# Attention scores of two batches on 32x64 TensorE tiles, probabilities turned in the score banks, row sum divided at the output's eviction

## The chip, the cores and the metric

The kernel runs on one core of a Trainium2 chip. The metric is the device time of one execution in microseconds. Five engines take part: TensorE (PE; its weight loads are PEld), VectorE (DVE), ScalarE (ACT), GpSimd (POOL) and SyncE (SP), each with its own queue of instructions, tied together by semaphores.

## The reference

Four residual steps on x of 128 batches x 32 tokens x 256 channels:

```python
x = x + einsum('bct,bcd->bdt', x, w0[cond])          # a 32x32 matrix for each batch
x = x + attention(x)                                 # paged keys and values, window of 128
x = x + einsum('bct,bcd->bdt', x, w2[subj])
x = x + x @ W.T + s[a] * (x @ A[a].T) @ B[a].T        # a = adapter of the batch
```

The attention has 8 query heads in 4 groups (G = 4, two heads a group), a head dimension of 32, and blocks of 16 keys:

```python
q, k, v = x @ Wq.T, x @ Wk.T, x @ Wv.T; q, k = rope(rms(q)), rope(rms(k))
k_blocks[blk, :, off] = k; v_blocks[blk, :, off] = v  # the new tokens are written first
scores = einsum('bghtd,bgsd->bghts', q, k_all[table]) * SCALE
allowed = (kpos <= pos) & (kpos > pos - WINDOW)
p = softmax(where(allowed, scores, -inf))
out = einsum('bghts,bgsd->bghtd', p, v_all) @ Wo.T
```

All of it is fp32. Only the 11 blocks that the window can touch are read, KEYS = 176 keys a batch.

## The kernel before

A first part (to about 118 us) works out indices on VectorE and GpSimd, applies w0, projects queries, keys and values of all 32 tiles (a tile is 4 batches x 32 tokens = 128 rows), spills x and q to memory, and scatters new keys and values into a buffer of written blocks. Then it gathers, in groups of 8 batches, old and newly written blocks (`gather_old`, `gather_new`, indirect DMAs of GpSimd).

The second part is a software pipeline written by hand. `run_slots` calls, on each engine, `slot(it, k)`: k runs from -8 to 138, with k = 8 to 23 as the body of a loop of six turns (16 slots each, a "pass" below), and the rest unrolled. Slot k works on batch k's scores, batch k-1's transposed probabilities, batch k-2's product with the values, and, by tables, on end steps of earlier tiles and preparation of the next group. On TensorE slot k is, in order:

- `s_exp` of batch k-2 awaited, then the scores of batch k: for each of two heads h of a group, one fp32 matmul of all 128 rows (4 groups x 32 dimensions) with a block-diagonal query `qbd` as weights (128 columns, 4 groups x 32 tokens), and one bf16 matmul of `mask_sel` with the penalty tile `pen` that adds the mask (L1328, L1329)
- one end step (`FIN`): x2 (output projection, slots 3 mod 4), x3 (w2, 0 mod 4), xa (adapter's A, 1 mod 4), x4 (W and B, 2 mod 4)
- four transposes of batch k-1's normalised probabilities into another bank (L1339)
- preparation (`PREP`): four transposes of keys (L1287, four times a group) or two of queries (L1279, twice a group)
- eight matmuls with the values for batch k-2, each 88 keys by a group's 32 columns, over 64 columns of probabilities (L1354); the four groups g write at four column tiles

An fp32 matmul is two records in the trace (L1328 has four of them a slot for two matmuls); a transpose is one.

VectorE in slot k takes the maximum of batch k (L704), copies keys, rotates queries, makes the penalty of the next tile (`make_pen`, in slots 3 mod 4, used from the next slot on), reorders gathered blocks, adds x2 (L735) or masks xa (L738, which x4 then waits for), and only then waits for the slot's exponentials, takes the reciprocal (L744) and scales the probabilities (L749, two instructions). ScalarE evicts the output (L1113) and the end steps, computes the two exponentials with their row sums (L1130), and copies the transposed probabilities out (L1143) and the turned queries into the block diagonal (L1153, four copies).

```python
PREP = {0: [("k0", None)], 1: [("k1", None)], 2: [("k2", None)], 3: [("qT", 0)], 4: [("k3", None)], 7: [("qT", 1)]}
FIN = {3: ("x2", 7), 0: ("x3", 8), 1: ("xa", 9), 2: ("x4", 10)}
```

`k0` waits for the gather of the newly written blocks (L871); SyncE's store of the values (L991) waits for the same gather. GpSimd starts the gather of a group in slot 1 of the group before, after the instruction `rstd` (L828), which VectorE's rotation of queries releases in slot 0 (L576).

## Time and profile before

| what | us |
|---|---|
| median of 3 runs | 558.14 |
| the three runs | 554.74, 558.14, 560.75 |
| span of the profiled execution | 556.0 |
| TensorE busy in it | 466.1 |
| VectorE busy | 413.0 |
| ScalarE busy | 341.7 |
| slot 0 starts on TensorE | 167.9 |
| last instruction of slot 127's scores | about 540 |

The profiled execution's own time is known by its span alone; the median of the runs lies 2.1 us over it. Busy time is a sum over all stages. The 128 slots between 168 and 540 us are two thirds of the span, so what a change of the slot is worth is read there.

### The profile page before, as it was taken

To read this page: it belongs to the slowest core of one execution; us is meant where nothing else is said; L and a number is where in the kernel's file an instruction comes from. 1 tells how busy PE (TensorE), PEld (TensorE's weight loads), DVE (VectorE), ACT (ScalarE), POOL (GpSimd) and SP (SyncE) were. 2 spreads that over 40 slices of the span, in tenths; PEclk is the share of its full clock that TensorE was granted. 3 is DMA by queue.
4 is the path that set the end of the run, shared out by engine and by line. 5 is a ranking of instruction groups with operands and counts; after the bars stand their busy time and mean duration, and the time that the engine had idled before them with its cause. 6 is when DMAs were issued, how large, how long until landed. Compare 5 with 4: busy or idle time off the path is not lost.

```text
span 556.0 us, 15369 instructions
## 1 busy us (share of the span) xinstructions
PE 466.1 (84%) x4726; PEld 386.1 (69%) x4726; DVE 413.0 (74%) x1357; ACT 341.7 (61%) x1075; POOL 205.6 (37%) x236
## 2 busy tenths in 40 slices
PE   0648899980015999999999999999999999999996
PEld 0537799970014688778778877877887887888884
DVE  7965577954116888888888878888888888788651
ACT  6238454455004677677777777768677775877662
POOL 7422588979603132332314324152331423211000
PEclk9999999995557899999999999999999999999999
DMA  7977776658266575757667596875858769645000
GB/s 231 293 271 306 242 219 203 201 176 199 67 155 144 146 179 150 171 142 182 155 132 179 129 174 159 151 175 124 181 139 134 182 144 182 153 127 128 13 21 19
DMA packets 97784, 90.09 MB, mean 162 GB/s; under 512 B 22967, under 2 KB 93655, under 8 KB 94972
## 3 DMA queue, kind: packets, MB, share of 16 engines
q1 hardware_dynamic: 82384, 52.58, 38.6%
q0 software_dynamic: 9312, 31.58, 22.1%
q10 hardware_dynamic: 6056, 5.54, 3.0%
q8 instruction: 16, 0.26, 0.2%
q14 instruction: 16, 0.13, 0.1%
HBM read 78.02 MB, written 35.65 MB: 204 GB/s over the span
## 4 chain that ended last, share of the span: by engine, by line
issue 47%; PE 12%; POOL 10%; DMA 3%; POOLq 1%; ACT 1%; DVE 0%; ACTq 0%; DVEq 0%
POOL old L862 4%; PE bank L1328 3%; DMA new<-written_blocks,g_idx 3%; POOL new L871 3%; POOL rms L828 3%; PE bank L1339 2%; PE bank L1354 2%; PE bank L1311 1%; POOL g_idx L855 1%; PE bank L1292 1%; PE bank L1306 1%; PE bank L1312 1%; PE bank L1329 1%; PE bank L1300 1%; PE bank L1287 0%
## 5 line engine op out<-in xcount | busy, mean ns | idle before, releaser
L828 POOL TENSOR_TENSOR rms<-rms,halfpow 128x8 f32<-128x8 f32 x48 | 86.1, 1793 | 247.4 <-DVE rms L576 247.4
L1130 ACT ACTIVATE p_room<-bank,nmax 128x176 f32<-128x176 f32 x256 | 101.4, 403 | 79.0 <-DVE nmax L704 74.9
L1328 PE MATMUL bank<-blocks_room,qbd 128*128 128x176 f32 x512 | 127.1, 352 | 6.6 <-issue 5.5
L1328 PEld LDWEIGHTS bank<-blocks_room,qbd 128*128 128x128 f32 x512 | 78.5, 193 | 26.6 <-issue 7.8
L1339 PE MATMUL bank<-ident,p_room 128*88 128x128 f32 x512 | 77.9, 275 | 4.8 <-DVE p_room L749 4.2
L704 DVE TENSOR_REDUCE nmax<-bank 128x2 f32<-128x352 f32 x128 | 66.6, 521 | 20.4 <-PE bank L1329 17.6
L1143 ACT ACTIVATE pT_room<-bank 88x512 f32<-88x512 f32 x128 | 75.1, 587 | 0.4 <-PE bank L1339 0.4
L749 DVE TENSOR_SCALAR p_room<-p_room,rrec 128x176 f32<-128x176 f32 x256 | 70.1, 316 | 5.6
L1339 PEld LDWEIGHTS bank<-ident,p_room 128*88 128x88 f32 x512 | 57.5, 123 | 15.9 <-DVE p_room L749 8.7
L712 DVE COPY blocks_room<-bank 128x352 f32<-128x352 f32 x64 | 47.5, 747 | 22.2 <-PE bank L1287 22.2
L1329 PE MATMUL bank<-pen,mask_sel 128*128 128x176 bf16 x256 | 61.9, 242 | 0.0
L1287 PE MATMUL bank<-ident,new 88*128 88x88 f32 x256 | 31.4, 249 | 34.3 <-DMA new<-written_blocks,g_idx 34.0
L1130 ACT ACTIVATION_READ_ACCUMULATOR p_room<-bank,nmax 128x1 f32 x256 | 51.5, 201 | 0.0
L1287 PEld LDWEIGHTS bank<-ident,new 88*128 88x128 f32 x256 | 26.7, 147 | 35.7 <-DMA new<-written_blocks,g_idx 35.0
L1153 ACT ACTIVATE qbd<-bank 32x256 f32<-32x256 f32 x128 | 47.4, 371 | 1.1
L1124 ACT ACTIVATE end_room<-bank 128x256 f32<-128x256 f32 x32 | 12.3, 383 | 57.8 <-PE bank L1312 57.8
L744 DVE RECIPROCAL rrec<-rsum 128x2 f32<-128x2 f32 x128 | 20.3, 159 | 34.1 <-ACT p_room L1130 33.7
L847 POOL DMA_INDIRECT written_blocks<-blocks_room,kv_idx x32 | 34.9, 1090 | 13.5 <-issue 13.5
L1311 PE MATMUL bank<-w3T,end_room 128*128 128x256 f32 x128 | 35.1, 397 | 1.8 <-DVE end_room L738 0.5
L1292 PE MATMUL bank<-woT,end_room 128*128 128x256 f32 x128 | 34.0, 388 | 0.6 <-ACT end_room L1124 0.6
L1231 PE MATMUL bank<-wkvT,pT_room 128*128 128x256 f32 x128 | 33.8, 388 | 0.0
L1077 ACT ACTIVATE blocks_room<-bank 128x256 f32<-128x256 f32 x32 | 12.3, 384 | 34.9 <-PE bank L1233 30.1
(199 smaller groups left out, 938.4 us busy)
## 6 DMA issues: line engine op xcount, KB each, us to landing
values_by_group<-new SPq DMA_DIRECT2D x16, 704.0 KB
blocks_room<-values_by_group SPq DMA_DIRECT2D x8, 704.0 KB
v_room<-values_by_group SPq DMA_DIRECT2D x8, 704.0 KB
xin<-in_x_dram SPq DMA_DIRECT2D x32, 128.0 KB
x_spill<-v_room SPq DMA_DIRECT2D x32, 128.0 KB
q_spill<-v_room SPq DMA_DIRECT2D x32, 128.0 KB
written_blocks<-new ACTq DMA_DIRECT2D x2, 2048.0 KB, 8.7
blocks_room<-q_spill SPq DMA_DIRECT2D x32, 128.0 KB
```

The source lines that it names most:

```text
L704: v.tensor_reduce(nmax[:, k % 4, :], ps_s[k % 2][:, 0:HPG * KEYS].rearrange("p (h k) -> p h k", h=HPG), AX.X, ALU.max, negate=True).then_i ...
L712: v.tensor_copy(kT[n % 2][:, :, :, o:o + 4].rearrange("p f w o -> p o f w"), ps_m[bank][:, 0:4 * ROWS].rearrange("p (o f w) -> p o f w", o ...
L749: last = v.tensor_scalar(pn[k % 2][:, h, :], pex[k % 2][:, h, :], rrec[:, k % 4, h:h + 1], None, ALU.mult)
L828: pool.tensor_tensor(out=rms[:, i, 2, :], in0=rms[:, i, 1, :], in1=halfpow[:, :], op=ALU.pow).then_inc(s_rstd, 1)
L1130: last = a.activation(pex[k % 2][:, h, :], ps_s[k % 2][:, h * KEYS:(h + 1) * KEYS], ACT.Exp, bias=nmax[:, k % 4, h:h + 1], accum_out=rsum[ ...
L1143: a.activation(pT[(k - 1) % 2][:, :, :, :].rearrange("p c h t -> p (c h t)"), ps_p[(k - 1) % 2][0:HK, :], ACT.Copy).then_inc(s_ptc, 1)
L1153: last = a.activation(qbd[n // 2 % 2][rows, TB * (n % 2):TB * (n % 2) + TB, :, C * g:C * g + C], m[rows, 0:HPG * 128].rearrange("p (h f t) ...
L1287: last = turn_over(m[:, ROWS * o:ROWS * o + ROWS], new[i][0:ROWS, o0 + o, 0, :], ident[0:ROWS, 0:ROWS])
L1311: mm(m[:, 0:T], x3T[n % 2][:, c, :], w3T[:, c, :], start=(c == 0), stop=False)
L1328: mm(dst, qbd[grp % 2][:, f, h, :], kT[grp % 2][:, f, :, :].rearrange("p w o -> p (w o)"), start=True, stop=False)
L1329: last = mm(dst, mask_sel[:, k % 4, :], pen[n % 2][:, :], start=False, stop=True)
L1339: last = turn_over(ps_p[(k - 1) % 2][0:HK, (HPG * c + h) * 128:(HPG * c + h + 1) * 128], pn[(k - 1) % 2][:, h, HK * c:HK * c + HK], ident[ ...
```

## The change

A slot no longer handles one batch with all four groups, but a *unit*: two batches (f2 = 0, 1) with two of the four groups (i = 0, 1; g = 2 (k mod 2) + i). Two slots still make two batches. Its parts:

- The query is kept compact (`qT`, 128 rows x 64 columns a batch) in place of the block diagonal. For each i and f2 one fp32 matmul works on a tile of 32 rows (the group's dimensions) and 64 columns (heads x tokens) at partitions 64 f2, in bank i of a pair of banks. The mask is added first, by two bf16 matmuls over the whole array.
- The four transposes of the unnormalised probabilities go back into the same pair of banks, which the scores no longer need. The scores of slot k+2 so wait for the copy out of these banks (`s_ptc`), where they waited for the exponentials.
- The scaling on VectorE is gone. Once in two slots it takes a reciprocal of four row sums and spreads it to 128 columns (`rrep`), TensorE turns that into half a bank (`s_nt`), ScalarE copies it (`norm`) once in four slots, and VectorE multiplies the output by it while evicting to `oT`.
- The matmuls with the values cycle over two column tiles a slot.
- The order in a slot: on TensorE the transposes now stand ahead of the end step, and on ScalarE copy and exponentials stand ahead of the end step's copies and the reordering. The memsets of `qbd` and the copies into the diagonal are gone (one copy of 128x256 in place of four of 32x256).

```diff
-        mask_sel = sb("mask_sel", [128, TB, 128], bf16)
+        mask_sel = sb("mask_sel", [128, 2, 128], bf16)
...
-        qbd = [sb(f"qbd{i}", [128, GB, HPG, 128]) for i in range(2)]
+        qT = [sb(f"qT{i}", [128, GB, HPG, C]) for i in range(2)]
...
-        rsum = sb("rsum", [128, 4, HPG])
-        rrec = sb("rrec", [128, 4, HPG])
-        ps = [ctx.enter_context(nc.psum_tensor(f"bank{i}", [128, 512], f32)) for i in range(8)]
-        ps_s, ps_p, ps_o, ps_m = ps[0:2], [ps[2], ps[4]], ps[5], [ps[6], ps[7], ps[3]]
+        rsum = sb("rsum", [128, 2, G])
+        rrec = sb("rrec", [128, 2, G])
+        rrep = sb("rrep", [128, 2, G * HD])
+        norm = [sb(f"norm{i}", [128, TB * HPG * C]) for i in range(2)]
+
+        ps_u = [ctx.enter_context(nc.psum_tensor(f"unit_banks{i}", [128, 2, 512], f32)) for i in range(2)]
+        ps = [ps_u[i // 2][:, i % 2, :] for i in range(4)] + [
+            ctx.enter_context(nc.psum_tensor(f"bank{i}", [128, 512], f32)) for i in range(4, 8)]
+        ps_o, ps_m = ps[5], [ps[6], ps[7], ps[4]]
+        NORM_AT = TB * HPG * C
...
@@ -701,8 +704,23 @@
                     make_pen(0, 0)
                 if 0 <= k < B:
                     dve.wait_ge(s_qk, b + 1)
-                    v.tensor_reduce(nmax[:, k % 4, :], ps_s[k % 2][:, 0:HPG * KEYS].rearrange("p (h k) -> p h k", h=HPG),
-                                    AX.X, ALU.max, negate=True).then_inc(s_max, 1)
+                    v.tensor_reduce(nmax[:, k % 4, :], ps_u[k % 2][:, :, 0:KEYS], AX.X, ALU.max, negate=True).then_inc(s_max, 1)
+                if k % 4 == 2 and 0 <= (k - 6) // 4 < NT:
+                    n = (k - 6) // 4
+                    dve.wait_ge(s_pv, 16 * it + 4 * n + 4)
+                    dve.wait_ge(s_ntc, 4 * it + n + 1)
+                    v.tensor_tensor(oT[n % 2][:, :, :, :].rearrange("p h f t -> p f h t"),
+                                    ps_o[:, 0:NORM_AT].rearrange("p (f h t) -> p f h t", f=TB, h=HPG),
+                                    norm[n % 2][:, :].rearrange("p (f h t) -> p f h t", f=TB, h=HPG), ALU.mult).then_inc(s_oc, 1)
+                if k % 2 == 0 and 0 <= (k - 2) // 2 < B // 2:
+                    j = (k - 2) // 2
+                    dve.wait_ge(s_exp, b)
+                    v.reciprocal(rrec[:, j % 2, :], rsum[:, j % 2, :]).then_inc(s_rec, 1)
+                    dve.wait_ge(s_rec, 8 * it + j + 1)
+                    if j >= 2:
+                        dve.wait_ge(s_nt, 8 * it + j - 1)
+                    v.tensor_copy(rrep[:, j % 2, :].rearrange("p (g d) -> p g d", g=G),
+                                  rrec[:, j % 2, :].unsqueeze(2).broadcast_to([128, G, HD])).then_inc(s_rrep, 1)
 
                 for kind, n in prep_steps(k) if k < 0 else prep_steps(k - 1) if k > 0 else []:
                     bank, _ = misc((kind, n), it)
...
-                if 0 <= k < B:
-                    dve.wait_ge(s_exp, b + 1)
-                    v.reciprocal(rrec[:, k % 4, :], rsum[:, k % 4, :]).then_inc(s_rec, 1)
-                    dve.wait_ge(s_rec, b + 1)
-                    if k >= 2:
-                        dve.wait_ge(s_pt, b - 1)
-                    for h in range(HPG):
-                        last = v.tensor_scalar(pn[k % 2][:, h, :], pex[k % 2][:, h, :], rrec[:, k % 4, h:h + 1], None, ALU.mult)
-                    last.then_inc(s_pn, 1)
 
...
-            for i in range(2):
-                make(pool.memset(qbd[i][:, :, :, :], 0.0))
-            assert made[0] == cmark_qbd
...
@@ -1110,8 +1116,27 @@
                 if k % 4 == 2 and 0 <= (k - 6) // 4 < NT:
                     n = (k - 6) // 4
                     act.wait_ge(s_pv, 16 * it + 4 * n + 4)
-                    a.activation(oT[n % 2][:, :, :, :].rearrange("p h f t -> p f h t"),
-                                 ps_o[:, 0:TB * HPG * C].rearrange("p (f h t) -> p f h t", f=TB, h=HPG), ACT.Copy).then_inc(s_oc, 1)
+                    act.wait_ge(s_nt, 8 * it + 2 * n + 2)
+                    if n >= 2:
+                        act.wait_ge(s_oc, 4 * it + n - 1)
+                    a.activation(norm[n % 2][:, :], ps_o[:, NORM_AT:2 * NORM_AT], ACT.Copy).then_inc(s_ntc, 1)
+                if 0 <= k - 1 < B:
+                    if k >= 3:
+                        act.wait_ge(s_pv, b - 2)
+                    act.wait_ge(s_pt, b)
+                    a.activation(pT[(k - 1) % 2].rearrange("p s c r -> p s (c r)"), ps_u[(k - 1) % 2][0:HK, :, 0:2 * 128],
+                                 ACT.Copy).then_inc(s_ptc, 1)
+                if 0 <= k < B:
+                    act.wait_ge(s_max, b + 1)
+                    if k >= 2:
+                        act.wait_ge(s_pt, b - 1)
+                    if k >= 4 and k % 2 == 0:
+                        act.wait_ge(s_rec, 8 * it + k // 2 - 1)
+                    for i in range(2):
+                        g = 2 * (k % 2) + i
+                        last = a.activation(pex[k % 2][:, i, :], ps_u[k % 2][:, i, 0:KEYS], ACT.Exp,
+                                            bias=nmax[:, k % 4, i:i + 1], accum_out=rsum[:, k // 2 % 2, g:g + 1])
+                    last.then_inc(s_exp, 1)
...
-                        for g in range(G):
-                            rows = slice(HD * g, HD * g + HD)
-                            last = a.activation(
-                                qbd[n // 2 % 2][rows, TB * (n % 2):TB * (n % 2) + TB, :, C * g:C * g + C],
-                                m[rows, 0:HPG * 128].rearrange("p (h f t) -> p f h t", h=HPG, f=TB), ACT.Copy, scale=SCALE)
-                        last.then_inc(s_empty[bank], 1)
+                        a.activation(qT[n // 2 % 2][:, TB * (n % 2):TB * (n % 2) + TB, :, :],
+                                     m[:, 0:HPG * 128].rearrange("p (h f t) -> p f h t", h=HPG, f=TB),
+                                     ACT.Copy, scale=SCALE).then_inc(s_empty[bank], 1)
...
@@ -1322,23 +1329,32 @@
                     if f == 0:
                         await_keys(pe, grp, it)
                     if k >= 2:
-                        pe.wait_ge(s_exp, b - 1)
-                    for h in range(HPG):
-                        dst = ps_s[k % 2][:, h * KEYS:(h + 1) * KEYS]
-                        mm(dst, qbd[grp % 2][:, f, h, :], kT[grp % 2][:, f, :, :].rearrange("p w o -> p (w o)"), start=True, stop=False)
-                        last = mm(dst, mask_sel[:, k % 4, :], pen[n % 2][:, :], start=False, stop=True)
+                        pe.wait_ge(s_ptc, b - 1)
+                    scores = ps_u[k % 2]
+                    for i in range(2):
+                        mm(scores[:, i, 0:KEYS], mask_sel[:, k // 2 % 2, :], pen[n % 2][:, :], start=True, stop=False)
+                    for i in range(2):
+                        rows = slice(HD * (2 * (k % 2) + i), HD * (2 * (k % 2) + i) + HD)
+                        for f2 in range(2):
+                            f = 2 * (k // 2 % 4) + f2
+                            last = mm(scores[HPG * C * f2:HPG * C * f2 + HPG * C, i, 0:KEYS],
+                                      qT[grp % 2][rows, f, :, :].rearrange("p h t -> p (h t)"),
+                                      kT[grp % 2][rows, f, :, :].rearrange("p w o -> p (w o)"), start=False, stop=True)
                     last.then_inc(s_qk, 1)
+                if 0 <= k - 1 < B:
+                    pe.wait_ge(s_exp, b)
+                    for i in range(2):
+                        for c in range(2):
+                            last = turn_over(ps_u[(k - 1) % 2][0:HK, i, 128 * c:128 * c + 128],
+                                             pex[(k - 1) % 2][:, i, HK * c:HK * c + HK], ident[:, :])
+                    last.then_inc(s_pt, 1)
+                if k % 2 == 1 and 0 <= (k - 3) // 2 < B // 2:
+                    j = (k - 3) // 2
+                    pe.wait_ge(s_rrep, 8 * it + j + 1)
+                    at = NORM_AT + 128 * (j % 2)
+                    turn_over(ps_o[:, at:at + 128], rrep[:, j % 2, :], ident[:, :]).then_inc(s_nt, 1)
                 for kind, n in fin_step(k):
                     misc_step(it, kind, n)
-                if 0 <= k - 1 < B:
-                    pe.wait_ge(s_pn, b)
-                    if k >= 3:
-                        pe.wait_ge(s_ptc, b - 2)
-                    for c in range(2):
-                        for h in range(HPG):
-                            last = turn_over(ps_p[(k - 1) % 2][0:HK, (HPG * c + h) * 128:(HPG * c + h + 1) * 128],
-                                             pn[(k - 1) % 2][:, h, HK * c:HK * c + HK], ident[:, :])
-                    last.then_inc(s_pt, 1)
...
-                    col = HPG * C * (kb % 4)
-                    for c in range(2):
-                        for g in range(G):
-                            last = mm(ps_o[HD * g:HD * g + HD, col:col + HPG * C], vg[kb // GB % 2][:, kb % GB, c, HD * g:HD * g + HD],
-                                      pT[kb % 2][:, c, :, C * g:C * g + C], start=(c == 0), stop=(c == 1))
+                    for f2 in range(2):
+                        f = 2 * (kb // 2 % 4) + f2
+                        col = HPG * C * (f % TB)
+                        for c in range(2):
+                            for i in range(2):
+                                g = 2 * (kb % 2) + i
+                                last = mm(ps_o[HD * g:HD * g + HD, col:col + HPG * C], vg[kb // GB % 2][:, f, c, HD * g:HD * g + HD],
+                                          pT[kb % 2][:, i, c, HPG * C * f2:HPG * C * f2 + HPG * C], start=(c == 0), stop=(c == 1))
                     last.then_inc(s_pv, 1)
```

How the orders stand. TensorE in the loop's body, slot 1 of a group, before: values of two slots back, scores, xa, transposes.

```order
L1354 MATMUL bank<-pT_room,blocks_room 32x64 [waits pT_copied]
L1354 MATMUL bank<-pT_room,blocks_room 32x64 x7
L1328 MATMUL bank<-blocks_room,qbd 128x176 [waits exp_done]
L1329 MATMUL bank<-pen,mask_sel 128x176
L1328 MATMUL bank<-blocks_room,qbd 128x176
L1329 MATMUL bank<-pen,mask_sel 128x176
L315 REGISTER_ALU
L1306 MATMUL bank<-end_room,abT 128x128 [waits end_empty]
L1306 MATMUL bank<-end_room,abT 128x128
L1334 REGISTER_ALU
L1339 MATMUL bank<-ident,p_room 88x128 [waits pT_copied,p_normal]
L1339 MATMUL bank<-ident,p_room 88x128 x3
```

The same place with the change:

```order
L1373 MATMUL bank<-pT_room,blocks_room 32x64 [waits pT_copied]
L1373 MATMUL bank<-pT_room,blocks_room 32x64 x7
L1335 MATMUL unit_banks<-pen,mask_sel 128x176 [waits pT_copied]
L1335 MATMUL unit_banks<-pen,mask_sel 128x176
L1340 MATMUL unit_banks<-blocks_room,qT 64x176 x4
L1345 REGISTER_ALU
L1348 MATMUL unit_banks<-ident,p_room 88x128 [waits exp_done]
L1348 MATMUL unit_banks<-ident,p_room 88x128 x3
L1353 ISA
L1355 MATMUL bank<-ident,rrep 128x128 [waits rec_spread]
L318 REGISTER_ALU
L1313 MATMUL bank<-end_room,abT 128x128 [waits end_empty]
```

The transposes moved ahead of xa (L1306, now L1313), wait for the exponentials themselves, and a transpose of `rrep` came in behind them.

VectorE, slot 2 of a group, from the maximum on, before:

```order
L703 REGISTER_ALU
L704 TENSOR_REDUCE nmax<-bank 128x2 [waits qk_done]
L712 COPY blocks_room<-bank 128x4x88 [waits prep_full1]
L588 REGISTER_ALU
L589 REGISTER_ALU [waits rope_op]
L591 TENSOR_TENSOR qr<-rp,rms 128x4x2x32 [waits rstd_ready]
L744 RECIPROCAL rrec<-rsum 128x2 [waits exp_done]
L749 TENSOR_SCALAR p_room<-p_room,rrec 128x176 [waits p_turned,rec_done]
L749 TENSOR_SCALAR p_room<-p_room,rrec 128x176
```

And with the change:

```order
L706 REGISTER_ALU
L707 TENSOR_REDUCE nmax<-unit_banks 128x2 [waits qk_done]
L711 REGISTER_ALU [waits pv_done]
L712 TENSOR_TENSOR end_room<-bank,norm 128x4x2x32 [waits norm_copied]
L718 RECIPROCAL rrec<-rsum 128x4 [waits exp_done]
L719 REGISTER_ALU
L721 REGISTER_ALU [waits rec_done]
L722 COPY rrep<-rrec 128x128 [waits norm_turned]
L730 COPY blocks_room<-bank 128x4x88 [waits prep_full1]
L591 REGISTER_ALU
L592 REGISTER_ALU [waits rope_op]
L594 TENSOR_TENSOR qr<-rp,rms 128x4x2x32 [waits rstd_ready]
```

Reciprocal and scaling at the slot's end are gone; behind the maximum stand now the output's multiply, a reciprocal of four sums and its spreading.

ScalarE, the slot with x4's copy, before:

```order
L311 REGISTER_ALU [waits out_done0]
L1124 ACTIVATE end_room<-bank 128x256 [waits end_full]
L1126 REGISTER_ALU
L1130 ACTIVATE p_room,rsum<-bank,nmax 128x176 [waits p_normal,max_done]
L1130 ACTIVATE p_room,rsum<-bank,nmax 128x176
L1143 ACTIVATE pT_room<-bank 88x512 [waits p_turned,pv_done]
```

And with the change:

```order
L1127 ACTIVATE pT_room<-unit_banks 88x512 [waits p_turned,pv_done]
L1130 REGISTER_ALU
L1137 ACTIVATE p_room,rsum<-unit_banks,nmax 128x176 [waits rec_done,p_turned,max_done]
L1137 ACTIVATE p_room,rsum<-unit_banks,nmax 128x176
L1147 ISA
L314 REGISTER_ALU [waits out_done0]
L1149 ACTIVATE end_room<-bank 128x256 [waits end_full]
```

x4's copy (L1124, now L1149), which waits for TensorE, stood ahead of the exponentials and now stands behind them.

## Rows read from the trace of the kernel before

**Rows 1.** The page: the span, and the busiest engine's line.

```profile
span 556.0 us, 15369 instructions
...
PE 466.1 (84%) x4726; PEld 386.1 (69%) x4726; DVE 413.0 (74%) x1357; ACT 341.7 (61%) x1075; POOL 205.6 (37%) x236
```

**Rows 2.** Stretches: one pass; length, then busy us of PE, PEld, DVE, ACT, POOL, clock, DMA.

```profile
264.60:311.55 46.95, 45.76 (x535) 37.65 (x529) 39.94 (x129) 34.67 (x117) 14.77 (x14) 1.00 0.67 153
```

**Rows 3.** Timeline of PE, 300 to 312 us: start, us, engine, line, operation.

```profile
301.80 0.60 PE L1339 MATMUL bank<-ident,p_room 128*88 128x128 f32 x4
302.24 0.47 PE L1287 MATMUL bank<-ident,new 88*128 88x88 f32 x4
302.64 0.43 PE L1354 MATMUL bank<-pT_room,v_room 88*32 88x64 f32 x16
303.00 0.57 PE L1328 MATMUL bank<-blocks_room,qbd 128*128 128x176 f32 x2
303.40 0.24 PE L1329 MATMUL bank<-pen,mask_sel 128*128 128x176 bf16 x1
303.48 0.50 PE L1328 MATMUL bank<-blocks_room,qbd 128*128 128x176 f32 x2
303.81 0.24 PE L1329 MATMUL bank<-pen,mask_sel 128*128 128x176 bf16 x1
303.89 0.64 PE L1306 MATMUL bank<-end_room,abT 128*128 128x128 f32 x4
304.37 0.60 PE L1339 MATMUL bank<-ident,p_room 128*88 128x128 f32 x4
304.90 0.43 PE L1354 MATMUL bank<-pT_room,v_room 88*32 88x64 f32 x16
...
306.07 0.24 PE L1329 MATMUL bank<-pen,mask_sel 128*128 128x176 bf16 x1
306.39 1.10 PE L1311 MATMUL bank<-w3T,end_room 128*128 128x256 f32 x4
...
307.76 0.60 PE L1339 MATMUL bank<-ident,p_room 128*88 128x128 f32 x4
...
309.54 1.06 PE L1292 MATMUL bank<-woT,end_room 128*128 128x256 f32 x4
310.44 0.60 PE L1339 MATMUL bank<-ident,p_room 128*88 128x128 f32 x4
```

**Rows 4.** Timeline of all engines, 273.4 to 277.9 us, ahead of slot 4's scores.

```profile
276.11 0.43 PE L1354 MATMUL bank<-pT_room,blocks_room 88*32 88x64 f32 x16
...
276.50 0.40 DVE L695 SCALAR_TENSOR_TENSOR pen<-keypos,tok_lo,pen_hi 128x176 bf16<-128x176 f32 x1
...
277.00 0.54 PE L1328 MATMUL bank<-blocks_room,qbd 128*128 128x176 f32 x2 [0.46 <-issue]
```

**Rows 5.** Timeline of DVE, 300 to 312 us: the masked xa.

```profile
305.96 0.28 DVE L738 TENSOR_TENSOR end_room<-bank,amask 128x128 f32<-128x128 f32 x1
```

**Rows 6.** Timeline of ACT, 300 to 324 us: exponentials, copy, what follows.

```profile
304.65 0.41 ACT L1130 ACTIVATE p_room<-bank,nmax 128x176 f32<-128x176 f32 x1 [1.01 <-DVE nmax L704]
...
305.33 0.20 ACT L1130 ACTIVATION_READ_ACCUMULATOR p_room<-bank,nmax 128x1 f32 x1
305.43 0.58 ACT L1143 ACTIVATE pT_room<-bank 88x512 f32<-88x512 f32 x1
305.90 0.38 ACT L1113 ACTIVATE end_room<-bank 128x256 f32<-128x256 f32 x1
```

**Rows 7.** The gather: L871's landings, its start, and who follows it.

```profile
DMA to landing us min/median/max: 11.3/14.3/16.1
...
298.11 1.06 POOL L871 DMA_INDIRECT new<-written_blocks,g_idx  x1 [1.03 <-issue]
...
313.19 0.95 SPq L991 DMA_DIRECT2D values_by_group<-new  x1
313.25 0.40 PEld L1287 LDWEIGHTS bank<-ident,new 88*128 88x128 f32 x4
```

**Rows 8.** Source line L819, GpSimd's memsets of qbd.

```profile
L819 POOL MEMSET qbd<- x2: 1804/1804/1804, 27.4 to 29.2; 128x2048 f32 x2
```

32 lines of the change are left out of this document (9 added, 23 removed).

## The prediction

> **What bounds the kernel now.** I read the span and the engines' shares first, then one pass of the attention loop, then its TensorE rows, then what the other engines do where TensorE is late. The span is 556.0 us and TensorE is the busiest engine [rows 1]. One pass of the loop handles 16 slots and takes 46.95 us, and TensorE is busy for 45.76 of it, at full clock [rows 2]. So a slot costs 2.93 us and TensorE nearly fills it; VectorE (39.94) and ScalarE (34.67) have room. Busy time hides small waits, since matmuls overlap in the records, so I count by starts instead [rows 3]:
>
> - scores of a batch: 303.00 to 303.89, 0.89 us (first fp32 pair 0.40, second 0.33, each bf16 mask 0.08)
> - four transposes of probabilities: 301.80 to 302.24, 0.44 us; before the values' matmuls it is 304.37 to 304.90, 0.53, so that going to 32-column tiles costs 0.09
> - values: 302.64 to 303.00, 0.36 us
> - xa 303.89 to 304.37, 0.48 (x3 is of the same form); x4 306.39 to 307.76, 1.37; x2 309.54 to 310.44, 0.90; a key step 302.24 to 302.64, 0.40 with the 0.09 in it, so 0.31; a query turn is two transposes, 0.22
>
> In a pass stand 16 x (0.89 + 0.44 + 0.09 + 0.36) = 28.5, 8 x 0.48, 4 x 1.37, 4 x 0.90, 8 x 0.31 and 4 x 0.22, together 44.8 us. The pass takes 46.95: **2.15 us are waits**. Two of them show: x4 starts 0.32 after the last mask instead of 0.08 [rows 3], as VectorE makes xam only at 305.96 [rows 5]; and the scores of slot 4 start 0.89 after the values instead of 0.36, right behind the penalty tile that VectorE began at 276.50 and held for 0.40 [rows 4]. VectorE is late because in each slot it stands waiting for that slot's exponentials before it may go on.
>
> **The change, part by part** (us per slot; there are as many slots as before, 128, each now half the heads of two batches).
>
> Scores. Two full fp32 matmuls and two masks become two masks and four fp32 matmuls on tiles of 32 rows by 64 columns. If the four run side by side, they take about one warm pair: masks 0.08 + 0.08, into tiles 0.09, one pair 0.33 with a few hundredths for the stagger less what a cold first load costs today, out again 0.09, in all 0.68 instead of 0.89: **-0.21**. No row of before shows a tile with fewer than 88 rows, so this is bounded: one after another, four pairs cost 4 x 0.33 = 1.32 and the stage 1.66 (+0.77, with the same switches); two side by side, +0.30 over my value. I take four, since the values' matmuls do it: 16 instructions of 64 columns, for which one pair in a full array would take about 0.12 (64/176 of 0.33), eight pairs 0.96, go by in 0.36 with the switch [rows 3]. They are four column tiles; two row groups by two column groups is the step that I assume.
>
> The Trainium skill (TensorEngine Tiling, Key Properties) says that changing the tiling mode drains TensorE. By that rule the change doubles the drains of a slot; the trace agrees (0.53 against 0.44), and it is the 0.09 twice that the sum above has.
>
> Values. The eight matmuls now cycle over two column tiles, not four. Two rounds of a pair become four, at 0.11 each (half of the 0.44 that four 128-column transposes take, over two): **+0.21**.
>
> Row sum. Four of VectorE's passes per two slots (reciprocal, twice two scalings) become a reciprocal and one copy; TensorE gets one more transpose per two slots, 0.11 / 2: **+0.06**. The scaling of the output moves from ScalarE's copy to a copy there and a multiply on VectorE, once in four slots, on engines with room.
>
> Order of loads. xa's four instructions take 0.48, the four transposes of equal width 0.44 [rows 3]: a weight load of fp32 can't hide behind a 0.08 mask. The end steps now stand behind the transposes: **-0.04**.
>
> Sum on TensorE: -0.21 + 0.21 + 0.06 - 0.04 = **+0.02** a slot, 0.3 a pass. The change hardly saves TensorE anything.
>
> Waits. What it can give is the 2.15. The scaling, which had to wait for the slot's exponentials, is off VectorE's queue; the maximum comes first in a slot and the reciprocal asks only for the slot before. VectorE loses two scalings and a reciprocal a slot and gains some 0.2: so the penalty and xam are early. x4 also stands behind the transposes now, 0.5 later. On ScalarE the query's four copies become one. New wait: the transposes need the exponentials themselves and write into the score banks, so that the next but one slot's scores wait for the copy out. That circle is exponentials 0.88 (304.65 to the copy at 305.43, and the accumulator's 0.10 behind it), transposes 0.60, copy 0.48 [rows 3, 6], with semaphores some 2.1 us; queued behind the transposes on TensorE are the end step, the key step and the values. The shortest slot has 0.89 + 0.48 + 0.53 + 0.36 = 2.26. It fits, with little over. ScalarE's other copies go into the gap between exponentials and the next copy. I take the 2.15 as gone; kept, the change costs 0.3 a pass.
>
> So a pass goes to 45.1, 1.85 less; over the seven passes' worth of slots that wait like this (the last 16 hardly do) **-13**.
>
> What is late next: the gather of newly written blocks. GpSimd starts it at 298.11, SyncE's store of its values waits for it and leaves at 313.19, and TensorE's key step starts at 313.25: it has landed at the last moment [rows 7]. It takes 11.3 to 16.1 us, median 14.3 [rows 7], and is started from VectorE's work early in a group, so it doesn't come earlier when slots shorten. Eight slots lose 0.93 us, and the key step stands 0.2 earlier in its slot: groups with a landing near the median or over it give all of it back as a wait, though a wait in one group is room for the next. I count half of the gain as lost: **+6**.
>
> Nothing for the zeroing of qbd: 3.6 us of GpSimd at 27.4 [rows 8], and GpSimd then idles until it is asked for the first rstd; with that cover gone it could cost 3.6 at most. Ahead of the loop the kernel is the same. The tail loses a scaling and gains a copy and a multiply, within 0.5.
>
> 556.0 - 13 + 6 = 549.0 of span. The three runs have their median 2.1 over the span, so the forecast is about **551.5 us**.
>
> **Rivals.**
>
> 1. *Two tiles at a time* (slower). Two row groups in the same columns don't run together. Price 0.30 a slot where TensorE sets the pace, 128 x 0.30 = 38, on a base that no longer has the gather's wait (-13): 558 + 25 = 583. It decides from 0.10 a slot on, a stage over 0.78 (128 x 0.10 = 13). For it: nothing in the trace has two row groups. One tile at a time gives +0.85 + 0.02 a slot against the waits' 0.13: about 650.
>
> The Trainium skill (TensorE: Matmul & The Clock Gate, Part 3) has matmuls start strictly in program order. An fp32 matmul is a pair here (two records each), and if the second of a pair holds up the next tile, four tiles take five halves, 0.74 instead of 0.33, which is +0.41 and 595 us. The values' rows speak against it: eight pairs so held up would take nine halves, about 0.5, and they take 0.36 with the switch. The same part gives 3.07 for four row tiles; 4 x 0.33 / 3.07 is 0.43, by which the gain would shrink by 0.10 a slot, to about nothing (an estimate from that page).
>
> 2. *The waits stay* or the circle binds. ScalarE or VectorE is late elsewhere, the gather takes back everything: 556 to 561.
>
> 3. *The gather doesn't bind.* Its landing gets faster or its start earlier, as VectorE is ahead: 551.5 - 6 = 545.
>
> **Chances.** Forecast, 548 to 555: 0.40. Waits stay, 555 to 563: 0.18. Gather free, 541 to 548: 0.14. Two at a time or held-up pairs, 575 to 595: 0.20, mostly under 588. One at a time: 0.04. Something between, 563 to 575: 0.04. One per cent, which is about what a measurement of this kernel can tell from no change, is 5.6 us: faster than 552.6 holds the gather's case and three quarters of the forecast's, 0.44; within it the rest and most of the waits', 0.27; slower 0.29. The range reaches from 543 to 587.
>
> **What would show it.** In the profile after: starts from the first mask to the transposes, 0.68 (0.98 with two tiles, 1.5 with one); values to the next mask 0.57; no gap at the masks of slots 4, 8 and 12; a pass of 45 to 46.2; a wait of the key step on the gather of 0.5 to 1 in every other group, which is absent now; ScalarE's idle time before the exponentials gone and found before the copy out of the score banks. I am wrong if TensorE waits for the exponentials at the transposes in most slots, if tiles are not side by side, or if the drain into the 32-row tiles is much over 0.09.

## Result and the profile after

The changed kernel takes **564.39 us** (median of 4 runs, 558.62 to 568.26) and the kernel before, run beside it, 556.44. The ratio is 1.0117, 95% interval 1.0063 to 1.017: **slower by 1.2%**, clear of no change, where 551.5 us and faster was forecast. Ratios, here and below, leave out runs over 1.5% above the fastest run of the same kernel (here the one of 568.26), and medians are over all runs. The profiled execution, the lowest of the four, has a span of 556.4 us against 556.0. The middle of the loop got faster, the first 16 slots and the last 16 slower.

The page of after, the engines' line and TensorE's granted clock in 40 slices, and under it the same clock line of before:

```profile
PE 480.4 (86%) x5302; PEld 368.4 (66%) x5302; DVE 363.8 (65%) x1133; ACT 309.3 (56%) x979; POOL 200.6 (36%) x234
...
PEclk9999899995555599999999999999999999999999
```

```profile
PEclk9999999995557899999999999999999999999999
```

VectorE lost 49 us of work and ScalarE 32, TensorE gained 14. Stretches of after, in the columns of [rows 2]: the first 16 slots, two passes of the loop, and the slots from 112 to the end of the last:

```profile
163.79:219.54 55.75, 51.71 (x532) 35.83 (x532) 33.86 (x97) 29.28 (x99) 14.43 (x14) 0.71 0.60 140
219.54:265.95 46.41, 46.15 (x605) 34.69 (x601) 34.28 (x100) 30.82 (x105) 14.51 (x14) 1.00 0.68 161
265.95:312.33 46.38, 46.14 (x603) 34.67 (x601) 34.29 (x100) 30.81 (x105) 14.51 (x14) 1.00 0.72 156
498.39:540.00 41.61, 41.61 (x550) 30.77 (x546) 22.88 (x68) 24.56 (x90) 3.48 (x2) 1.00 0.22 52
```

The same first and last stretches of the kernel before:

```profile
167.87:217.55 49.68, 43.23 (x460) 34.77 (x460) 39.21 (x125) 31.96 (x107) 14.63 (x14) 0.90 0.64 160
...
499.29:539.90 40.61, 40.52 (x485) 33.53 (x479) 27.86 (x92) 27.14 (x98) 3.48 (x2) 1.00 0.22 54
```

So a pass went from 46.95 [rows 2] to 46.38, 0.57 less and not 1.85; the tail costs 1.0 more; and the first 16 slots cost 6.1 more, at a clock of 0.71 instead of 0.90. (The slots begin 4 us earlier in this one execution. Over all profiles below they begin anywhere from 163.5 to 169 us in kernels of both kinds, so nothing is built on that.) From slot 0 to the end it is 392.6 us against 388.1, 4.5 more: +6.1 for the first 16 slots, -2.9 for the six passes together, +1.0 for the last 16 slots, +0.3 behind them.

Timeline of TensorE in after, one slot and a half, against [rows 3]:

```profile
303.15 0.64 PE L1373 MATMUL bank<-pT_room,v_room 88*32 88x64 f32 x16
303.72 0.33 PE L1335 MATMUL unit_banks<-pen,mask_sel 128*128 128x176 bf16 x2
303.98 0.53 PE L1340 MATMUL unit_banks<-blocks_room,qT 32*64 32x176 f32 x8
304.44 0.64 PE L1348 MATMUL unit_banks<-ident,p_room 128*88 128x128 f32 x4
304.91 0.27 PE L1355 MATMUL bank<-ident,rrep 128*128 128x128 f32 x1
305.02 0.61 PE L1313 MATMUL bank<-end_room,abT 128*128 128x128 f32 x4
305.56 0.64 PE L1373 MATMUL bank<-pT_room,v_room 88*32 88x64 f32 x16
```

Read starts, not durations. Scores run from 303.72 to 304.44, 0.72 us (before 0.89). The four tiles are side by side: two fp32 instructions each, all eight within 0.46 us with the switch back to the full array. Values take 303.15 to 303.72, 0.57 (0.36 before). The transposes take 304.44 to 304.91, 0.47 (0.44 before): the first full-width load behind the small tiles is not hidden. The row sum's transpose is 0.11, and the xa step, now behind transposes, 305.02 to the values' matmuls with no bubble but 0.09 of switch.

Who waits for whom in the loop of after (page's part 5: busy, mean ns, then idle before and its releaser):

```profile
L1127 ACT ACTIVATE pT_room<-unit_banks 88x512 f32<-88x512 f32 x128 | 75.9, 593 | 130.9 <-PE unit_banks L1348 130.8
L707 DVE TENSOR_REDUCE nmax<-unit_banks 128x2 f32<-128x352 f32 x128 | 67.1, 524 | 101.7 <-PE unit_banks L1340 101.4
L1137 ACT ACTIVATE p_room<-unit_banks,nmax 128x176 f32<-128x176 f32 x256 | 99.8, 395 | 34.6 <-DVE nmax L707 34.6
```

VectorE's and ScalarE's idle time now ends with TensorE. TensorE's own waits in the six passes after the first are these two (total, times, longest):

```profile
PE unit_banks L1335 <- issue: 1.3, 5, 0.3
PE bank L1294 <- DMA new<-written_blocks,g_idx: 0.2, 1, 0.2
```

What is left is the wait at the loop's branch, 0.27 a pass, and one late gather: the third pass, with it, took 46.99. So the waits are gone, as forecast, and the time went into TensorE's own work: TensorE is busy for 46.14 of a pass of 46.38.

### The profile page after: what moved, and what is told of

It reads as the page before. It is cut to its first block, busy times and chain, and to the rows that moved or that the text cites. A ratio compares the mean times of both kernels' runs of the same rounds, so it can differ in the third digit from the quotient of the medians.

```text
span 556.4 us, 16229 instructions
## 1 busy us (share of the span) xinstructions
PE 480.4 (86%) x5302; PEld 368.4 (66%) x5302; DVE 363.8 (65%) x1133; ACT 309.3 (56%) x979; POOL 200.6 (36%) x234
## 4 chain that ended last, share of the span: by engine, by line
PE 38%; issue 27%; POOL 6%; DMA 3%; POOLq 0%; DVE 0%; ACT 0%; DVEq 0%; ACTq 0%
PE bank L1373 8%; PE unit_banks L1348 7%; PE unit_banks L1340 6%; PE unit_banks L1335 3%; PE bank L1318 3%; PE bank L1299 3%; DMA new<-written_blocks,g_idx 3%; POOL old L868 2%; PE bank L1294 2%; PE bank L1313 2%; PE bank L1307 2%; POOL new L877 2%; PE bank L1319 1%; POOL rms L834 1%; PE bank L1355 1%
## 5 line engine op out<-in xcount | busy, mean ns | idle before, releaser
L1127 ACT ACTIVATE pT_room<-unit_banks 88x512 f32<-88x512 f32 x128 | 75.9, 593 | 130.9 <-PE unit_banks L1348 130.8
L707 DVE TENSOR_REDUCE nmax<-unit_banks 128x2 f32<-128x352 f32 x128 | 67.1, 524 | 101.7 <-PE unit_banks L1340 101.4
L1137 ACT ACTIVATE p_room<-unit_banks,nmax 128x176 f32<-128x176 f32 x256 | 99.8, 395 | 34.6 <-DVE nmax L707 34.6
L1348 PE MATMUL unit_banks<-ident,p_room 128*88 128x128 f32 x512 | 84.7, 290 | 0.0
L1348 PEld LDWEIGHTS unit_banks<-ident,p_room 128*88 128x88 f32 x512 | 50.7, 126 | 34.0 <-issue 27.8
L1340 PE MATMUL unit_banks<-blocks_room,qT 32*64 32x176 f32 x1024 | 70.2, 345 | 0.0
L1137 ACT ACTIVATION_READ_ACCUMULATOR p_room<-unit_banks,nmax 128x1 f32 x256 | 50.3, 197 | 0.0
L1373 PE MATMUL bank<-pT_room,blocks_room 88*32 88x64 f32 x1024 | 43.6, 231 | 3.2 <-DMA blocks_room<-values_by_group 3.1
L1335 PE MATMUL unit_banks<-pen,mask_sel 128*128 128x176 bf16 x256 | 43.0, 251 | 3.1 <-issue 1.3
L1373 PE MATMUL bank<-pT_room,v_room 88*32 88x64 f32 x1024 | 41.0, 222 | 0.1
```

The source lines that it names most:

```text
L707: v.tensor_reduce(nmax[:, k % 4, :], ps_u[k % 2][:, :, 0:KEYS], AX.X, ALU.max, negate=True).then_inc(s_max, 1)
L1127: a.activation(pT[(k - 1) % 2].rearrange("p s c r -> p s (c r)"), ps_u[(k - 1) % 2][0:HK, :, 0:2 * 128], ACT.Copy).then_inc(s_ptc, 1)
L1137: last = a.activation(pex[k % 2][:, i, :], ps_u[k % 2][:, i, 0:KEYS], ACT.Exp, bias=nmax[:, k % 4, i:i + 1], accum_out=rsum[:, k // 2 % 2, ...
L1335: mm(scores[:, i, 0:KEYS], mask_sel[:, k // 2 % 2, :], pen[n % 2][:, :], start=True, stop=False)
L1340: last = mm(scores[HPG * C * f2:HPG * C * f2 + HPG * C, i, 0:KEYS], qT[grp % 2][rows, f, :, :].rearrange("p h t -> p (h t)"), kT[grp % 2][ ...
L1348: last = turn_over(ps_u[(k - 1) % 2][0:HK, i, 128 * c:128 * c + 128], pex[(k - 1) % 2][:, i, HK * c:HK * c + HK], ident[:, :])
```

## Experiments

All ratios are to the kernel before on the same chip. They were taken on several chips, each beside runs of the kernel before. Three edits recur. **Clock held**: 39 extra fp32 matmuls of 512 columns into a bank not in use, most where TensorE waits for the first gathers, three at slot 2. It doesn't hold the clock throughout: the mean over the first 16 slots is 0.87 to 0.90 in the eight kernels with this edit, and 0.71 to 0.73 in changed kernels without it.

```diff
+            def keep_busy(n):
+                for _ in range(n):
+                    mm(ps_m[2][:, 0:512], ident[:, :], abT[:, :, :].rearrange("p c t -> p (c t)"), start=True, stop=True)
...
+                if k == -6:
+                    keep_busy(9)
+                    pe.wait_ge(s_order[0], 8)
+                    keep_busy(5)
...
+                if k == 2:
+                    keep_busy(3)
```

**Paired values**: pT has four buffers, and every second slot runs the values of two batches over four column tiles in turn.

```diff
-                if 0 <= k - 2 < B:
-                    kb = k - 2
+                if 0 <= k - 3 < B and k % 2 == 1:
+                    kb = k - 3
...
                         for c in range(2):
-                            for i in range(2):
-                                g = 2 * (kb % 2) + i
+                            for g in range(G):
```

**Old blocks first**: on GpSimd, in slots 0 and 8 of a pass, the two gathers of old blocks stand ahead of the power that waits for VectorE.

```diff
+                kk = k + EARLY
+                i, j, grp = (kk // 8) % 2, kk % 8, kk // 8 + 2
+                if j == 3 and k >= 0 and grp + 1 < NG:
+                    gather_old(1 - i, 2 * it + grp + 1)
                 for n in rotated_tiles(k):
                     rstd(rope_of_tile(4 * it + n), n % 2)
```

### First four: the clock, the order, the values

> The changed kernel with 39 fp32 matmuls of the identity by 512 columns into an idle bank, on TensorE alone, in the 40 us in which it waits for the first gathers, and in slot 2; output unchanged. Theory (the clock): the loop's pass got shorter by 0.56 us, seven passes, some 4 us, and the kernel is slower only since its first eight slots run at half the clock (up to 196.7 us, before 185.0). With the clock held the first 16 slots take under 50 us instead of 55.75, and the time falls by 6 to 10 us, to about the time of the kernel before or below. Rival (the slots themselves are slower in a way that the profiled execution, the fastest of four, doesn't show): no more than 2 us less.

> The same 39 matmuls in the kernel before. Theory (the clock): it gains less than the changed kernel does, 2 to 5 us, since its clock was back at 171 and again at 185 us; with both held at full clock the changed kernel is 3 to 5 us faster than the one before. Rival: both gain the same, and the changed kernel stays 1% slower.

> The kernel before with only the order of the change: on TensorE the transposes ahead of the end step, on ScalarE copy and exponentials ahead of the end step's copies and the reordering. Theory: the waits of x4 (0.64 us a pass) and the slow first load of the end steps (0.7 us a pass) go, the waits for the penalty tile stay or shrink, so a pass goes from 46.95 to 45.5 to 46.3 and the time 3 to 8 us down. Rival: the transposes now wait for the scaled probabilities, which VectorE has ready late, and the pass gets longer, over 47.5.

> The changed kernel, but the values' matmuls of two units are done together in every other slot, in an order that cycles over four column tiles, from four buffers of transposed probabilities instead of two. Theory: the stage costs 0.42 + 0.15 + 0.09 us a slot now; together it costs 0.42 + 0.15 + 0.09 in two slots, so TensorE's work falls by 0.3 us a slot, 5 us a pass. If TensorE sets the pace alone a pass takes 41.5 us; if the gather of written blocks is next (landing 14.3 us after its start, which hangs on slot 0 of its group), a pass stops at 44 to 45 and the key step waits for it. The time falls by 12 to 35 us. Rival: TensorE didn't set the pace, and the pass stays at 46.

Clock held, changed kernel: 559.38, ratio **1.0082** [1.004, 1.0123]. Clock held, before: 555.08, **1.0009** [0.9977, 1.0042]. The first 16 slots of the changed kernel fell from 55.75 to 48.51 us, which should have been worth 1.3%, and the ratio fell by 0.35%, some 2 us, which is the rival's number. With both clocks held the changed kernel is still 0.7% slower, where 3 to 5 us faster was expected. The trace shows a part of why. Timeline of TensorE, in the third pass behind the first 16 slots, which took 51.35 us where the other five took 46.4 to 47.5:

```profile
333.55 0.61 PE L1307 MATMUL bank<-bd,end_room 128*128 x4
336.17 0.85 PE L1294 MATMUL bank<-ident,new 88*128 88x88 f32 x4 [2.01 <-DMA new<-written_blocks,g_idx]
336.95 1.07 PE L1389 MATMUL bank<-pT_room,blocks_room 88*32 88x64 f32 x16
```

and the stretches from slot 56's start to the end of the wait, and behind it:

```profile
332.37:336.17 3.80, 1.79 (x18) 1.20 (x18) 2.50 (x8) 2.66 (x9) 0.91 (x1) 0.92 0.40 99
336.17:342.89 6.72, 6.72 (x61) 5.11 (x61) 2.21 (x6) 1.67 (x7) 4.41 (x6) 0.54 0.55 128
```

A gather that landed 17.6 us after its issue (median 14.4) stopped TensorE for 2.0 us, and then the clock was at its half level (0.54 granted over 6.72 us) though TensorE was busy throughout. Together slots 56 and 57 took 10.28 us instead of 5.32. So this late gather cost its wait and more than as much again in clock. The Trainium skill (TensorE: Matmul & The Clock Gate, in the section on HAM oscillation) says that waits for DMA between stretches of matmuls put the clock back; the trace agrees, with the two rows above, for a wait shorter than those of its example. The kernel before, clock held, had a wait at the same slot (1.68 us between two starts that are otherwise 0.11 apart) and a pass of 49.45 there. Not each such wait does it: two shorter ones of the same profile of the changed kernel, 0.85 us at 409 and 0.41 at 479, were followed by a clock of 1.00.

The order alone, in the kernel before: 581.71, **1.0494** [1.0439, 1.055], passes of 49.80. My first theory of a small gain fell; the rival held, and by more than it said:

```profile
PE bank L1337 <- DVE p_room L749: 17.4, 45, 0.6
PE bank L1328 <- ACT p_room L1126: 2.4, 5, 0.5
```

With scaled probabilities to wait for, transposes directly behind the scores stand and wait. Taking the scaling out is what makes the order pay.

Paired values: 541.21, **0.9663** [0.9574, 0.9752]. The ratio rests on the two lowest of six runs; by the medians of all it is 0.976. The gather now binds in every pass, 16.0 us in all (in the profile, which is of the longest of the six runs):

```profile
PE bank L1295 <- DMA new<-written_blocks,g_idx: 16.0, 6, 4.5
```

and after four of the six waits the clock fell to half. Its runs lie between 532.14 and 552.85.

### Second four: the wrong gather moved

> The changed kernel with the clock held (the 39 extra matmuls of the first experiment) and, on GpSimd in the slots, the gather of written blocks issued ahead of the two gathers of old blocks instead of behind them. Theory (clock and gather): what the changed kernel lost is the half clock in its first 16 slots and, with the clock held there, late gathers that stop TensorE for about 2 us and are followed by half clock again (slots 56, 57, 80). The gather is then issued about 3.5 us earlier, no key step waits for it, all passes of the loop take 46.4 us, the first 16 slots 48.5; from the first slot on 3.4 us less than the kernel before, ratio 0.994. Rival (something else costs 5 us, code or loads or the other engines): ratio 1.005 or more with passes of 46.4.

> The kernel before with the same two edits, clock held and the gather of written blocks first. Theory (clock and gather): passes 46.6 us, no gather waits, ratio 0.996 to 0.998, so that the change itself, with clock and gather out of the account, is worth 1 to 2 us. Rival: the gathers were never late here, ratio 1.000, and the change costs as much with these two held as without.

> The changed kernel with only the gather of written blocks issued first, the clock left alone. Theory (clock and gather): the first 16 slots still run at half clock, 55.7 us, the later passes are 46.35; ratio 1.008, about 0.4% below the changed kernel. Rival (gathers don't matter): 1.012.

> The changed kernel with values for two batches in one stage (four column tiles in turn) and the gather of written blocks issued first. Theory (clock and gather): the key step of every other group no longer waits 2 to 5 us and the clock is not lost behind it, clean passes of 42.2 us, ratio 0.94. Rival (the gather's landing is bound by the transfers in flight and not by its issue): its landing moves little, waits of 2 us stay, ratio 0.965 as without the move.

```diff
-                if j == 3 and k >= 0 and grp + 1 < NG:
-                    gather_old(1 - i, 2 * it + grp + 1)
                 if j == 4 and k > 0 and grp < NG:
...
                     gather_new(i, 2 * it + grp, 8 * fills + 8)
+                if j == 4 and k > 0 and grp + 1 < NG:
+                    gather_old(1 - i, 2 * it + grp + 1)
```

None of the four gained: **1.0126** [1.0072, 1.018] against 1.0082 without the move, **1.024** [1.0172, 1.0308] against 1.0009, **1.0196** [1.0131, 1.0261] against 1.0117, **1.0041** [1.0004, 1.0077] against 0.9663. The second and the fourth are slower beyond doubt, the intervals of the other two pairs overlap. From slot 16 on no key step waited for written blocks any more; they landed 6 to 12 us ahead of it, and in the first of the four 10.0 to 14.0 us after their issue (median 12.1). The old ones were now late. Waits of TensorE and of ScalarE in the passes of the first of these (changed kernel, clock held):

```profile
PE unit_banks L1349 <- DVE pen L698: 5.8, 8, 1.5
...
ACT new L1154 <- DMA old<-in_L_cond_v_blocks_dram,g_idx: 16.6, 10, 2.8
```

ScalarE and VectorE stand at the reordering of old blocks, the penalty is queued behind it on VectorE, and the next tile's masks on TensorE wait for the penalty. My theory was half right: the gathers cost time, but both kinds had no slack, and GpSimd's order only chose which was late. What was left was to start both earlier: GpSimd idles some 9 us in slot 0 and 8, waiting for VectorE, with the old gathers queued behind that wait and the new one behind them.

### Third four: old blocks first

> The changed kernel with the clock held (39 extra matmuls) and, on GpSimd in the slots, the two gathers of old blocks moved ahead of the power of slot 0 and 8, which waits 9 us for VectorE, so that they are issued some 9 us earlier and the gather of written blocks 3.5 us earlier. Theory (both gathers run without slack): no key step waits for written blocks, no piece of the reordering for old ones; first 16 slots 48.5 us, every later pass 46.35, tail 41.6; 3.4 us less than the kernel before from the first slot on, ratio 0.994. Rival (transfers slow one another): the old blocks in flight push the written ones back, waits stay, ratio 1.005 or more.

> The kernel before with the same two edits. Theory: first 16 slots 50.3 us, passes 46.5, tail 40.6, ratio 0.997; with clock and gathers out of the account the change is worth 1 to 2 us, and not the 6.6 that were forecast, since TensorE's own work grew by 0.08 us a slot and not by 0.02. Rival: ratio 1.000, as with the clock alone held.

> The changed kernel with values for two batches in one stage, old blocks gathered first, clock left alone. Theory: no waits for gathers, passes of 42.2 us, the first 16 slots 47.4 at half clock, ratio 0.94. Rival (transfers slow one another): 0.965, as without the move.

> The same with the clock held as well. Theory: the first 16 slots fall from 47.4 to about 42 us, ratio 0.93. Rival (the clock falls later instead, behind some wait): no better than without the held clock.

For the gathers this held. Changed kernel, clock held: 555.08, **0.9929** [0.9878, 0.998]. Before, clock held: 555.98, **1.0012** [0.9977, 1.0048], the rival's number. GpSimd in the first of these, around one group:

```profile
286.24 1.83 POOL L834 TENSOR_TENSOR rms<-rms,halfpow 128x8 f32<-128x8 f32 x1 [6.05 <-DVE rms L579]
288.05 0.32 POOL L861 COPY g_idx<-rd_idx 88x1 int32 x1
289.40 1.11 POOL L877 DMA_INDIRECT new<-written_blocks,g_idx  x1 [1.03 <-issue]
297.97 1.84 POOL L834 TENSOR_TENSOR rms<-rms,halfpow 128x8 f32<-128x8 f32 x1 [7.46 <-DVE rms L579]
299.78 0.18 POOL L861 COPY g_idx<-rd_idx 88x1 int32 x1
300.93 1.12 POOL L868 DMA_INDIRECT old<-in_L_cond_k_blocks_dram,g_idx  x1 [0.97 <-POOL g_idx L861]
```

The written blocks are asked for 3.2 us after the power starts, instead of 6.7, and land after 8.9 to 15.3 us, median 11.2, instead of 14.4, with no gather of old blocks just ahead of them in the queue. From slot 16 on no gather is waited for, the clock stays at 1.00, and six passes lie between 46.08 and 46.42 us. One pass of each, the changed kernel and the one before:

```profile
259.98:306.37 46.39, 46.15 (x604) 34.68 (x600) 34.29 (x100) 30.64 (x105) 14.96 (x14) 1.00 0.65 156
```

```profile
263.62:310.12 46.50, 45.70 (x535) 37.65 (x529) 39.92 (x129) 34.75 (x117) 14.78 (x14) 1.00 0.66 156
```

The first 16 slots of the same two runs, where 48.5 and 50.3 were expected; the clock is the same:

```profile
163.92:213.57 49.65, 46.20 (x538) 31.73 (x538) 33.74 (x97) 29.16 (x99) 14.96 (x14) 0.88 0.66 150
```

```profile
165.81:217.00 51.19, 45.81 (x466) 35.55 (x466) 39.14 (x125) 31.88 (x107) 14.54 (x14) 0.88 0.64 146
```

**The change itself is worth 0.11 us a pass** when the gathers are out of the account and the clock is the same. By the two profiles it is 0.8 us less from slot 0 to the end: 1.5 less in the first 16 slots, 0.5 less in the six passes, 1.2 more behind them. The ratios give 0.9929 / 1.0012 = 0.992, some 4.6 us, but 0.9929 rests on five of twelve runs, those up to 554.32, because one run took only 546.48; the granted clock of the seven left out (0.980 to 0.988) is that of the five (0.981 to 0.988). Over all twelve runs of each the medians are 555.08 and 555.98, 0.9 us apart, as the profiles have it. So a gain of about 1 us is what the record bears out, and more is not shown.

Paired values, old blocks first: 525.90, **0.9323** [0.9256, 0.9391], and with the clock held too 525.47, **0.9473** [0.9424, 0.9523]. The first ratio rests on two of six runs (514.85 and 519.72; the others took 525.7 to 526.9). By the medians of all runs the two are 0.946 and 0.946. Passes are 42.03, with no wait for a gather:

```profile
260.25:302.28 42.03, 41.67 (x607) 31.10 (x600) 34.04 (x100) 30.33 (x105) 15.54 (x14) 1.00 0.72 171
```

Holding the clock gave less than the theory's 42 us here: the first 16 slots took 47.20 instead of 49.60, and the timed runs don't show even that.

### Last three: each loss by itself

> The changed kernel with the old blocks gathered first and the clock left alone. Theory (two separate losses): the first 16 slots run at half clock and take 55 us or so, all later passes 46.4 without gather waits; ratio 1.004 to 1.009, against 0.993 with the clock held too and 1.012 for the change as it is. Rival (the gathers are the whole loss): 0.993 to 0.998, the clock in the first slots is worth little where those slots wait for the first gathers anyway.

> The kernel before with the old blocks gathered first and nothing else. Theory: passes 46.5 instead of 46.95, first 16 slots 49.7 as they are, ratio 0.995 to 1.001; the gathers cost this kernel little, and the changed one more, because the same landing meets shorter slots. Rival (the gathers cost both the same): this falls by as much as the changed kernel does.

> The changed kernel with clock held and old blocks first, and one part of the change undone: the end steps stand ahead of the transposes again on TensorE, and their copies ahead of the exponentials and the copy out of the banks on ScalarE. Theory (the part's whole worth is 0.04 a slot of load time, and the waits it moves are small): passes 46.4 + 0.7 = 47.1, ratio 1.00 to 1.01 against 0.993. Rival (the order carries the change): ScalarE's copies ahead of the exponentials make TensorE wait at the transposes of every slot with an end step, passes over 48.5, ratio over 1.03.

Old blocks first and nothing else: changed kernel 559.55, **1.0044** [1.0014, 1.0074]; before 556.25, **0.9972** [0.9952, 0.9992]. Taken in this order, the gathers are worth 0.7% to the changed kernel (1.0117 to 1.0044) and the clock 1.15% (1.0044 to 0.9929). Taken the other way round, the clock is worth 0.35% (1.0117 to 1.0082) and the gathers 1.5%. By the medians of all runs the clock is worth 0.5% or 0.3%, and the gathers 1.2% or 1.0%. The profiles, from slot 0 to the end, have 392.6 us for the changed kernel, 391.4 with either edit alone and 385.7 with both. So the two losses are there, but they aren't separate: with the clock held alone, late gathers took its gain back. How the loss divides isn't settled. For the kernel before, old blocks first is worth 0.3% alone and nothing with the clock held (1.0009 and 1.0012), and the held clock nothing. The first 16 slots of the two, changed kernel and before, where the half clock is left alone:

```profile
165.20:220.53 55.33, 50.98 (x531) 35.39 (x531) 33.61 (x97) 29.45 (x99) 15.07 (x14) 0.72 0.61 145
```

```profile
169.01:219.55 50.54, 44.54 (x461) 35.58 (x461) 39.26 (x125) 31.91 (x107) 14.94 (x14) 0.86 0.68 159
```

The old order put back, with clock held and old blocks first: 573.05, **1.0281** [1.0238, 1.0325], passes of 48.1 to 49.4. Neither theory had it right; it lies between the two, nearer to the rival. Not the transposes wait but the masks, for the copy out of the score banks. Two loads of masks, and then the transposes and the copy ahead of the first:

```profile
337.44 0.11 PEld L1347 LDWEIGHTS unit_banks<-pen,mask_sel 128*128 128x128 bf16 x2 [0.33 <-ACT pT_room L1135]
...
340.87 0.11 PEld L1347 LDWEIGHTS unit_banks<-pen,mask_sel 128*128 128x128 bf16 x2 [0.40 <-ACT pT_room L1135]
```

```profile
336.10 0.60 PE L1362 MATMUL unit_banks<-ident,p_room 128*88 128x128 f32 x4
336.80 0.59 ACT L1135 ACTIVATE pT_room<-unit_banks 88x512 f32<-88x512 f32 x1
```

With the end step ahead of the transposes, the copy comes behind both: it ends at 337.39, and the next slot's masks, which write into the same banks, start at 337.45. A slot without such a wait still takes 0.06 more. So the change needs the order: without it the rest is 3.5% slower than with it by the ratios (1.0281 / 0.9929), 2.7% by the medians of all runs.

## Why the prediction was wrong

Point by point, as it was put:

- **Four tiles side by side**: right. It priced the stage at 0.68; it is 0.71 to 0.72 by the rows, 0.03 to 0.04 more. Rival 1 is out, and with it the held-up pairs: in the trace the first four of the eight instructions start within 0.02 us, the other four 0.20 us later. (Two sums of these rivals were off: with their own terms held-up pairs give about 597 and not 595, and one tile at a time, 1.66 - 0.68 = 0.98 over the priced stage and not 0.85, gives about 670 and not 650. Nothing hung on either.) The estimate that the prediction worked out from the Trainium skill's 3.07 for four row tiles (TensorE: Matmul & The Clock Gate, Part 3) was 0.10 over 0.68, so the measured stage lies between. The Trainium skill's rule that a change of tiling mode drains the array (TensorEngine Tiling, Key Properties) was in the sum at 0.09 each way; the trace agrees for the values' switch, 0.09 (a key step ahead of the values takes 0.40, by itself 0.31). Not in the sum was that the transposes behind the small tiles begin with an unhidden load: 0.47 instead of 0.44.
- **Values +0.21, row sum +0.06**: right, 0.57 and 0.11 every second slot.
- **Order of loads -0.04**: right for the end steps, and given back by the transposes' load just named. **Sum +0.02 a slot**: mis-sized, and the first step that failed. A pass was 44.8 of work and 2.15 of waits; it is 46.11 of work and 0.27 of waits (the loop's branch), so the work grew by 1.3 a pass, **0.08 a slot**. The rows of one slot give the same: 0.04 more for the scores' stage than priced and 0.03 for the transposes behind it. Over the 128 slots the 0.06 that the forecast didn't have is 8 us.
- **Waits of 2.15 gone**: right, down to 0.27. But the gain left over in the loop is 0.57 a pass and not 1.85, and 2.9 us over the six passes. In the tail, where no waits stood before, the 0.08 shows bare: +1.0, where "within 0.5" was said.
- **Gather gives back +6**: in the profiled execution it gave back hardly 0.5, as the slots shortened less than forecast. By the timed runs the gathers cost the changed kernel 0.7 to 1.5% and the one before 0 to 0.3%. The mechanism was right, and one link of it was missing: behind a long wait the clock can fall to half. That is seen in both kernels with the clock held and in the one with paired values; the profile of the changed kernel itself has no such wait in its passes, so how often it met one in the timed runs isn't known.
- **"over the seven passes' worth of slots that wait like this"**: this is the step that failed and turned a small gain into a loss. The first 16 slots are the first of the seven, and they take 6.1 us more, not 1.85 less. With old blocks first, 5.7 us of them come back when the clock is held (55.33 to 49.65); the timed runs give 0.3 to 1.15% for it. The prediction took one pass at full clock as standing for all of them, while the page of before that it started from shows a clock of 0.5 up to where the slots begin and 0.7 and 0.8 in the slices behind it. Slots 3 to 7 in after, and slots 3 to 7 before:

```profile
176.36:196.34 19.98, 19.92 (x168) 12.95 (x167) 9.79 (x28) 8.78 (x30) 1.78 (x1) 0.50 0.52 124
```

```profile
180.10:194.60 14.50, 13.28 (x146) 10.19 (x143) 11.16 (x37) 9.10 (x32) 1.78 (x1) 0.83 0.58 153
```

TensorE enters both kernels' slots at the lower level, 1.2 GHz, after a stretch in which it mostly waited for the first gathers. In after:

```profile
124.90:163.79 38.89, 3.58 (x19) 2.66 (x20) 12.13 (x32) 4.80 (x10) 20.13 (x25) 0.50 0.57 137
```

Before, the level goes up in slot 1, falls again behind waits of 1.5 to 1.9 us in slots 1 and 2, and goes up for good within slots 3 to 7:

```profile
171.30:178.20 6.90, 3.12 (x25) 2.32 (x24) 6.61 (x20) 4.63 (x14) 4.55 (x6) 0.99 0.59 121
```

After, it stays down through 20 us in which TensorE is hardly idle in the records. The rise is as late in each kernel with the change's score tiles and no held clock: 0.71, 0.72 and 0.73 over the first 16 slots in after and the two with a gather moved. In these and in the three with paired values the level goes up only in or behind slot 7's output projection (x2), the first end step of full matmuls of 256 columns. The kernel before has 0.90, and the ones of it with old blocks first and with the other order 0.86 and 0.89. The values' two column tiles are not the reason: paired values, with four in turn, have the same clock. The first 16 slots with paired values, without and with old blocks first:

```profile
167.71:215.14 47.43, 45.53 (x532) 30.98 (x532) 33.87 (x97) 29.05 (x99) 14.43 (x14) 0.73 0.66 161
168.61:218.21 49.60, 46.65 (x532) 31.56 (x532) 33.49 (x97) 29.12 (x99) 14.90 (x14) 0.71 0.68 157
```

What is left is above all the scores' stage, 32x64 tiles in place of full matmuls. Whether the small tiles or the missing full ones matter, or the different waits ahead of them, wasn't tried apart and stays open.

Sum of it, from slot 0 to the end of the two profiles: forecast were -13 and +6; measured are +6.1 for the first 16 slots at the lower clock, -2.9 for the six passes with 0.08 a slot in place of 0.02, +1.3 behind them. The timed ratio gives 6.5 us, 2 more than this sum, and that difference isn't explained.

## What to carry to other kernels

Before one pass is multiplied by the number of passes, look at the granted clock of the stretches that aren't in the middle: work made of small tiles ran 20 us at half clock where the kernel with full matmuls had come out of it. When TensorE nears 99% of a pass, list what is waited for just in time (here two kinds of gathers on one queue, both behind an engine's wait): a shorter slot doesn't turn into time until they start earlier, and moving one ahead of the other only changes which is late. Column tiles pay only if enough of them are in turn: two at a time cost 0.21 a slot over four, and pairing two batches' values got it back, which with old blocks first made passes of 42.03 instead of 46.4 and 0.946 of the kernel before by the medians of all runs. And when a ratio leaves runs out, look at what it is over all of them: here one low run made 0.993 out of 0.999.
